# A twelve-stage decoder on one core: the opening, the second attention and the context layer rewritten together

## The reference, cut to what matters

```python
x = ln(x + self_attention_16_heads_of_64(x))                  # bf16 weights, rope
x = ln(x + cross_attention(x, ctx_1024, ctx_1024))            # 16 heads of 8 features
x = ln(x + soft_mixture_of_experts(x))
x = ln(x + gated_delta_rule(x))
x = ln(x + context_layer(x, ctx_1024, ctx_1024))
x = ln(x + picked_experts(x))

# cross attention (the "second attention")
wq, wk, wv = (q @ wq_w.T + wq_b), (k @ wk_w.T + wk_b), (v @ wv_w.T + wv_b)
scores = einsum('bthd,bshd->bhts', wq, wk) / sqrt(8)
attn = einsum('bhts,bshd->bthd', softmax(scores), wv) @ wo_w.T + wo_b

# context layer: both weights are the sequence's own context
h = einsum('eth,efh->etf', x, ctx);  y = einsum('etf,efh->eth', gelu(h), ctx)
```

## Time and profile before

| | us |
|---|---|
| median of 3 runs | 2493.59 (2485.16 to 2495.51) |
| profiled execution, its own time | 2487.64 |
| its span in the trace | 2485.9 |
| busy PE / DVE / ACT / POOL | 2215.4 / 1468.2 / 1091.5 / 559.9 |

### The profile page before, as it was taken

One profiled execution on the slowest core, in us unless ns is written; L12 is line 12 of the kernel. 1 busy time (PEld: TensorE's weight loads), 2 busy tenths in 40 slices (PEclk: granted clock), 3 DMA queues, 4 the chain that ended last, 5 costly groups with the idle time before them and its releaser, 6 DMA issues. The chain is left out here.

```text
span 2485.9 us, 95498 instructions
## 1 busy us (share of the span) xinstructions
PE 2215.4 (89%) x42219; PEld 1631.8 (66%) x42219; DVE 1468.2 (59%) x3213; ACT 1091.5 (44%) x1901; POOL 559.9 (23%) x582
## 2 busy tenths in 40 slices
PE   4999998689997679788999989999899997987998
PEld 2566666478873568127888878878788885455545
DVE  6888786345547754685666656666566665354213
ACT  0233334344447775674444435444344443243324
POOL 3656554011103100402222212212122222000100
PEclk7999999766568999888999989999899998986898
DMA  3000000000000000100000000000000001002001
GB/s 87 2 3 2 2 2 2 5 1 0 0 1 13 0 1 1 29 1 3 4 5 4 4 4 4 4 4 4 4 4 4 4 4 49 1 0 68 1 0 34
DMA packets 28107, 22.89 MB, mean 9 GB/s; under 512 B 11705, under 2 KB 22657, under 8 KB 27746
## 3 DMA queue, kind: packets, MB, share of 16 engines
q1 hardware_dynamic: 27298, 17.24, 2.6%
q0 software_dynamic: 448, 0.14, 0.1%
HBM read 15.28 MB, written 2.10 MB: 7 GB/s over the span
## 5 line engine op out<-in xcount | busy, mean ns | idle before, releaser
L1790 PE MATMUL psum<-dr_kq,dr_kSq 64*64 64x64 f32 x6144 | 226.5, 226 | 24.0 <-issue 18.5
L1790 PEld LDWEIGHTS psum<-dr_kq,dr_kSq 64*64 64x64 f32 x6144 | 206.0, 140 | 58.0 <-issue 54.6
L2207 POOL TENSOR_TENSOR dr_kSq<-dr_kSq,dr_decay 128x256 f32<-128x256 f32 x128 | 111.6, 872 | 443.7 <-PE psum L1790 443.7
L1796 PE MATMUL psum<-dr_G,dr_CT 64*64 64x32 f32 x5120 | 189.1, 224 | 1.0 <-issue 1.0
L2119 ACT ACTIVATE dr_Y<-psum 128x256 f32<-128x256 f32 x160 | 63.1, 394 | 284.2 <-PE psum L1796 284.2
L1790 PE MATMUL psum<-dr_GT,dr_Y 64*64 64x32 f32 x5120 | 184.3, 221 | 3.1 <-issue 3.1
L1790 PEld LDWEIGHTS psum<-dr_GT,dr_Y 64*64 64x64 f32 x5120 | 166.5, 136 | 11.1 <-issue 7.4
L1796 PEld LDWEIGHTS psum<-dr_G,dr_CT 64*64 64x64 f32 x5120 | 171.3, 137 | 1.1 <-issue 1.1
L1796 PE MATMUL psum<-dr_Y,dr_GT 64*64 64x32 f32 x4096 | 149.6, 222 | 18.8 <-issue 18.8
L1796 PEld LDWEIGHTS psum<-dr_Y,dr_GT 64*64 64x64 f32 x4096 | 134.1, 136 | 47.4 <-issue 41.3
L2362 DVE TENSOR_TENSOR dr_CT<-psum,dr_minus_masks 128x256 f32<-128x256 f32 x192 | 77.9, 419 | 100.7 <-PE psum L1790 100.7
(11 more groups left out here) (407 smaller groups left out, 5733.5 us busy)
## 6 DMA issues: line engine op xcount, KB each, us to landing
topk_w<-in_L_ffn_w_dram SPq DMA_DIRECT2D x16, 256.0 KB, 5.4
out_dram<-store_rows SPq DMA_DIRECT2D x4, 512.0 KB, 3.6
dout_w<-in_L_attn_Wff_dram SPq DMA_DIRECT2D x3, 256.0 KB, 3.2
attn_w_rows<-in_L_attn_Wq_dram SPq DMA_DIRECT2D x1, 256.0 KB, 3.2
attn_w_rows<-in_L_attn_Wk_dram SPq DMA_DIRECT2D x1, 256.0 KB, 4.0
attn_w_rows<-in_L_attn_Wv_dram SPq DMA_DIRECT2D x1, 256.0 KB, 5.2
attn_w_rows<-in_L_attn_Wo_dram SPq DMA_DIRECT2D x1, 256.0 KB, 6.0
moe_w<-in_L_ffn_w_dram SPq DMA_DIRECT2D x1, 256.0 KB, 3.4
```

The costliest lines, as they stand in the source:

```text
L1790: last = nc.tensor.matmul(out(r), lhsT(r), rhs(r), start=True, stop=True)
L1796: last = nc.tensor.matmul(out(HALVES[1 - j]), lhsT(r), rhs(r), start=True, stop=True)
L2207: pool.tensor_tensor(ks, ks, total.unsqueeze(2).to_broadcast([P, HB * (LR >> l), 1 << l]), ALU.mult).then_inc(kS_scaled[l], 1)
```

## The change

Three sets of edits. **Opening:** `load_tokens` is gone; x comes in four DMAs inside `attn_w`, all small loads and the context move to SP behind the weights, and the work on x is spread: DVE copies, ACT casts the first part, POOL makes the first subtraction, DVE the rest; ACT copies the weights. **Second attention:** one block in place of three ahead of the loop, with the context turned group by group between the projections, each bank released on its own. In the loop the values become the stationary operand (64x32) and the turned exponentials stream (256 columns), once against v and once against a tile of ones, which leaves sums with features on the partitions; ACT makes the inverse as exp(-ln); the output is four matmuls with a masked copy of Wo; q and v are copied by POOL. **Context layer:** one unrolled block in which turning of group g+1, first product of g and second product of g-1 follow each other, without the copies, and with the gelu table loaded once.

```diff
 attn_w, in after.py's order on each engine
+            for c in range(4):
+                sync.dma_start(x_rows[:, c * XC:(c + 1) * XC, :], x[:, c * XC:(c + 1) * XC, :]).then_inc(x_loaded[c], 16)
...
+                    sync.dma_start(bias_col[:, 2 * n, :], col).then_inc(small_loaded, 16)
...
+            sync.dma_start(k.ctx_rows[:, :, :],
+                           k.a["ctx_1024"].rearrange("(n u) t d -> (u t) n d", u=2)).then_inc(k.ctx_loaded, 16)
...
+                pool.tensor_tensor(first[g % 3][:, :], group(k.X, g), group(w.parts[:, 0, :], g), ALU.subtract
+                                   ).then_inc(first_left, 1)
...
+                act.activation(group(w.parts[:, 0, :], g), group(k.X, g), ACT.Copy).then_inc(first_part, 1)
...
+                act.activation(dst, half_bank[n][:, 0:AD], ACT.Copy).then_inc(kept, 1)
...
 xproj, PE
+                for g in range(NG):
+                    if g == 1:
+                        pe.wait_ge(ob_ready, 1)
+                    project(g)
+                    if g < NG - 2:
+                        turn_ctx(g + 2)
...
 the loop of the second attention
         def pe_turn(pe, t, c):
             pe.wait_ge(exp_ready[c], t + 1)
+            if c == 1:
+                pe.wait_ge(probsT_ready[0], t + 1)
+            elif later(t, 1):
+                pe.wait_ge(probsT_ready[1], t)
...
-            for g in range(GH):
-                for h2 in range(2):
-                    for j in range(2):
-                        for b in range(2):
-                            r, h = slice(b * T, (b + 1) * T), 4 * (GH * c + g) + 2 * h2 + j
-                            last = nc.tensor.matmul(V_BANK[r, h, :],
-                                                    probsT[c][r, g, h2 * TT + j * T:h2 * TT + (j + 1) * T],
-                                                    v_t[u][r, h, :], start=True, stop=True)
+                if later(t, 1):
+                    pe.wait_ge(mixed_kept, t)
+            for at, weights in ((slice(0, W), lambda r, g: v_t[u][r, 32 * g:32 * g + 32]),
+                                (slice(W, 2 * W), lambda r, g: ones[r, :])):
+                for g in range(GH * c, GH * (c + 1)):
+                    for b in range(2):
+                        r = slice(b * T, (b + 1) * T)
+                        last = nc.tensor.matmul(k.psum[32 * g:32 * g + 32, 5 + b, at], weights(r, g),
+                                                probsT[c][r, g - GH * c, :], start=True, stop=True)
...
+            for n in range(4):
+                last = nc.tensor.matmul(OUT_BANK, wo[:, n, :], mixed[:, n, :, :].rearrange("p b t -> p (b t)"),
+                                        start=(n == 0), stop=(n == 3))
...
+            act.activation(log_total[:, :, :], TOTAL, ACT.Ln).then_inc(log_ready, 1)
+            act.wait_ge(log_ready, t + 1)
+            act.activation(inverse[:, :, :], log_total[:, :, :], ACT.Exp, scale=-1.0).then_inc(inverse_ready, 1)
...
 context layer, PE
+            pe.wait_ge(k.ctx_loaded, 32)
+            turn_ctx(0)
+            for g in range(NG):
+                if g < NG - 1:
+                    turn_ctx(g + 1)
+                hidden(g)
+                if g >= 1:
+                    output(g - 1)
+            output(NG - 1)
```

More of the change, by code:

```diff
@@ L73, in block @@
         return self.stack.enter_context(self.nc.Block())
[L76 to L114, removed]
@@ L117, in turn_context @@
[L117 to L137, removed]
@@ L234, in attention_weights @@
     with Stage(k, "attn_w") as t:
+        x_rows = t.sb("x_rows", [P, NT, D])
         rows = t.sb("rows", [P, 4, NR, P], BF16)
         eye = t.sb("eye", [P, P], BF16)
-        left = t.sb("left", [P, 2, N // 2])
+        first, second = ([t.sb(f"{n}{u}", [P, G]) for u in range(3)] for n in ("first_left", "second_left"))
         bias_col = t.sb("qk_bias_col", [P, 4, NR], BF16)
@@ L301, in _, with keep @@
[L301 to L309 removed]
+            def keep(g):
+                dve.wait_ge(x_turned, g + 1)
+                dve.tensor_copy(group(k.X, g), k.bank[g][:, :]).then_inc(x_kept, 1)
@@ L310, in _ @@
+            for i in range(NG + 3):
+                if i < NG:
+                    keep(i)
+                if 2 <= i < NG + 2:
+                    split(i - 2)
+                if i >= 3:
+                    split_rest(i - 3)
             dve.wait_ge(small_loaded, 16 * 14)
@@ new lines, in _ @@
+                pe.wait_ge(k.ctx_loaded, 16)
+                turn_ctx(0)
+                turn_ctx(1)
+                pe.wait_ge(w_loaded, 64)
+                for i in range(4):
+                    last = nc.tensor.transpose(v_bank[1][:, i * D:(i + 1) * D], w_rows[:, i, :], k.eye[:, :])
+                last.then_inc(w_turned, 1)
+                pe.wait_ge(w_kept, 1)
+                pe.wait_ge(bias_loaded, 64)
+                nc.tensor.matmul(v_bank[1][:, 0:1], wT[:, 3, :], bias[:, 2:3], start=True, stop=True).then_inc(wobv_ready, 1)
@@ L702, in _ @@
                 dve.wait_ge(wobv_ready, 1)
[L703 to L710 removed]
+                dve.tensor_tensor(o_bias[:, :], v_bank[1][:, 0:1], bias[:, 3:4], ALU.add).then_inc(ob_ready, 1)
+                for g in range(NG):
+                    if g < NG - 2:
+                        keep_ctx(g + 2)
+                    keep_v(g)
             @block.scalar
@@ new lines, in hidden @@
+            def hidden(g):
+                pe.wait_ge(ctx_kept, g + 1)
+                if g >= 2:
+                    pe.wait_ge(gelu_ready, g - 1)
+                for n in range(H):
+                    for half in range(2):
+                        c = (2 * n + half) * T
+                        last = nc.tensor.matmul(h_bank[g % 2][half * T:half * T + T, n * T:(n + 1) * T],
+                                                ctx_g[g % 2][:, c:c + T], k.X[:, g * G + c:g * G + c + T],
+                                                start=True, stop=True)
+                last.then_inc(h_ready, 1)
@@ new lines, in output @@
+            def output(g):
+                pe.wait_ge(gelu_ready, g + 1)
+                if g >= 2:
+                    pe.wait_ge(added, g - 1)
+                for n in range(H):
+                    for half in range(2):
+                        r = slice(half * T, half * T + T)
+                        last = nc.tensor.matmul(y_bank[2 * (g % 2) + half][:, n * T:(n + 1) * T],
+                                                k.ctx_rows[r, H * g + n, :], hid[g % 2][r, n, :], start=True, stop=True)
+                last.then_inc(y_ready, 1)
@@ L2697 @@
+            for g in range(NG):
+                act.wait_ge(h_ready, g + 1)
+                if g >= 2:
+                    act.wait_ge(y_ready, g - 1)
+                act.activation(hid[g % 2][:, :, :].rearrange("p n t -> p (n t)"), h_bank[g % 2][:, 0:H * T],
+                               ACT.Gelu_apprx_tanh).then_inc(gelu_ready, 1)
 FE, FK, FH = 8, 16, 512
```

363 lines of the change are left out of this document (188 added, 175 removed).

## The result

The changed kernel takes 2407.33 us (median of 4 runs, 2397.93 to 2415.23), the kernel before beside it 2489.38 (4 runs, 2483.97 to 2495.51): a ratio of 0.9664, 95% interval 0.9628 to 0.970, faster by 82 us. The profiled execution took 2415.23 us, the longest of the four; its span is 2413.5 against 2485.9, the mean granted clock 0.94 against 0.90. So the two traces lie 72.4 us apart where the medians lie 82 apart.

What follows compares the result with a forecast made beforehand. PE was taken as the bound, its clock down at 0.59 in the second attention's loop. Opening, projections, loop and context layer gave 2487.64 - 15 - 17 - 30 - 10 = 2416 us, overall range 2396 to 2462 (some 0.83).

Steps and rivals of the forecast that it cites:

- its likeliest case: Whole kernel: the forecast of 2416 us, with a range of its own of 2398 to 2436; chance 0.70.
- the signs put down as right: Changed profile: first projection 29.5, projections' PE waits under 1 us, loop clock above 0.9, steps 5.7, L801 1.1, context layer 30.
- Loop, -30: Second attention's loop: full clock after a first step at the lower, 32 steps of 5.7 us, 186 for 216 us.
- the "wrong" mark of 0.3: Second attention's loop: PE waiting for ACT's L892 by more than 0.3 us a step would show the prediction wrong.
- Opening, -15: Opening: x turned earlier, weights queued behind x, work spread over engines; first projection at 29.5, 15 us earlier.
- the third rival: Parts other than the loop give little, -20 in place of -42, ending at 2438 us; chance 0.10.
- my other bound: Opening: if small loads or the context's issue hold SP, the first projection starts at 33 (-12 us).
- Projections, -17: Context, weights and projections: barriers and waits go, PE work stays, 36 us in place of 52.7.
- Context layer, -10: Context layer: one stream without holes, clock taken as up for more than half, 30 us in place of 39.8.
- The clock that stays down: Second attention's loop: 9.2 us a step, +78, ending at 2524; chance 0.07 for the slow end, 0.08 the middle.
- Only two tiles side by side: Loop's new values: two of four tiles run together, 58 us more, 2474, chance 0.04; none, 2576, chance 0.01.
- the rule on weight loads: Loop's values: the skill says weight loads overlap matmuls only in another row group, so column tiles would not run together.

Runs made afterwards that it cites:

- the control: Eight unread products of 9 columns a step added to the second attention's loop of the kernel before: ratio 1.0498, loop 332.4 us.
- POOL at rest: The changed kernel with the first subtraction of each group of x moved from POOL to DVE: ratio 0.9709, first projection at 34.08.
- the products in its first three groups: The changed kernel with two unread products of 256 columns a group in the context layer's first three groups: ratio 0.9646, layer 22.1 us.
- the kernel with the long product: The kernel before with one unread product of 256 columns a step in the second attention's loop: ratio 0.9849, loop 176.9 us.

## Why the prediction was right, point by point

The forecast was 2416 (2396 to 2462), the result 2407: its likeliest case, inside its own range of 2398 to 2436. The main mechanism, the loop's clock, was right. That the sum came so near is in part luck: the four terms were off by +6, -2, -5 and +3 us, which cancel, and of the signs put down as right three failed (first projection at 35.3 for 29.5, a PE wait of 1.36 us in the projections, the context layer 33.2 for 30).

- **What bounds the kernel** (the loop's clock decides): right, and stronger than put. The old loop with its clock up takes 176.9 us; the rewrite at the same level is slower a step (5.67 against 4.99). That added work of any kind would do it is refuted by the control; that it is the long rows in the rewritten loop too is argued from this, and no run takes them out of it.
- **Loop, -30, measured -35.4.** The clock came up as forecast; the size came out of terms that cancel. The four tiles run side by side, 1.07 for 1.08 forecast. The scores take 0.91 for 1.22: the earlier trace rows, called a stretch at the full clock, is not one for them. The window of before over them has 0.50:

```profile
554.40:555.70 1.30, 1.30 (x66) 1.15 (x65) 0.00 (x0) 0.75 (x2) 0.00 (x0) 0.50 0.00 0
```

  So the scores do grow at the lower level (1.29 against 0.91), against what the prediction says. PE waits 0.52 a step for L892 where I had 0.1, so that the "wrong" mark of 0.3 was passed; L892 stands behind logarithm and inverse in ACT's order, and moving it gave 0.32 a step back. Output 1.16 for 1.02.
- **Opening, -15, measured -9.2.** The step that failed is DVE's group of 1.9 us with the addition of 2.4 for hand-offs (2.2 a group with it). It took 2.95, since a cast beside POOL's subtraction takes 1.38, and with POOL at rest 2.72 with one subtraction of some 0.6 more; I had this as a bound without a size ("if POOL and DVE do not hinder each other, 27"), and the hindrance as the third rival. ACT's weight copies come late because they stand behind the last casts of x, which wait for DVE. SP did not hold it, against my other bound. The prediction's own terms end at 24 + 3.54 + 1.1 = 28.6, not at its 29.5; the 35.3 lies outside its bounds of 27 and 33.
- **Projections, -17, measured -18.9.** 34.8 us for 36 forecast, PE's work 28.7 for 31 and 6.0 idle for 5. Of the idle, 1.36 us for the weights' DMA and 0.96 for the biases' lie at the start; the largest part, 3.71, lies at the end, where the loop's first scores wait for POOL's first `kx` (L869). The prediction doesn't name that wait; the kernel before has the same one (3.7 us, for L851).
- **Context layer, -10, measured -6.8.** The step "the list loses its holes, so I take the clock as up for more than half" failed. The holes went, the clock stayed at 0.50, and the layer took the lower level's sum (4.00 us a group for 4.3 forecast) and no more. With the products in its first three groups, and the clock up behind them, it is 22.1 us in place of 31.7.
- **Not foreseen:** the first attention with its norm is 5.2 us shorter at nearly the same code, at a clock of 1.00 against 0.98 before. With the new opening alone in the kernel before it took 412.8 us, and with the old opening, in the kernel with the long product, 413.3: over all traces it is 412.5 to 415.3 in the kernels made from the one before, and 410.1 to 413.4 in the changed kernel and those made from it. Some of the 5.2 is spread between executions, the rest I did not try.
- **The rivals.** The clock that stays down: true in the context layer, not in the loop. Only two tiles side by side: refuted by 1.07. The other parts give little: true in its half on POOL; together they gave 35 us of the 42. That column tiles would not run together by the rule on weight loads was the prediction's own inference, and the 1.07 refutes it, as the earlier trace rows had.

## What to carry to other kernels

Where PE bounds a stage, read its granted clock before its work. A gapless list of short products can sit at the lower level for the whole stage, and then a few unread products with long rows, even in its first groups alone, can be worth as much as a rewrite in its place: 0.9849 against 0.9844 in the loop. Test by adding the work, with short products as the control, and look at every stage's clock again in the final kernel: the old loop's fell from 0.97 to 0.88 when other stages changed. Before a two-input operation goes to POOL, look which of DVE's casts and subtractions in SBUF it will lie beside. DVE's copy out of PSUM (0.68 to 0.69 us) and ACT's casts (0.63) kept their times beside POOL's work here.

## What was not expected of the hardware

- The same list of the context layer runs at 0.50 for its whole 31.7 us, or at 1.00 for the 12 us that were left of it, by the products ahead of it (4.00 or 2.24 us a group).
- Sixteen records of 128x128 weights and 9 columns take 3.58 us at the lower level and 2.04 at a clock of 0.95; eight of 64x256 on four tiles take 0.64.
- A float32 to bf16 cast of 128x512 in SBUF on DVE is 0.41 us, two-input subtraction 0.69, and beside a subtraction of POOL (1.33 us) the cast is 1.38; a cast of the same shape on POOL, 0.61 us, takes 1.01 where it lies beside DVE's subtraction, and the next subtraction then 1.09.
